# Rows of u and B in the product operands: 3 partitions apart over both halves, loaded 36 at a time

## The reference

```python
def step(h, ins):
    x_t, dt_t, B_t, C_t = ins
    dA = jnp.exp(dt_t[..., None] * A)
    h = dA * h + dt_t[..., None] * B_t[:, None, :] * x_t[..., None]
    y_t = jnp.einsum('ben,bn->be', h, C_t)
    return (h, y_t)
```

## Time and profile before

| | us |
|---|---|
| median of 3 runs | 1169.29 (1166.89 to 1173.1) |
| profiled execution | 1161.89 |
| its span | 1160.1 |
| busy: PE / DVE / ACT / POOL | 1013.9 / 936.7 / 910.1 / 845.2 |
| first update of the state (L1226) starts at | 182.4 |
| last update starts at | 1131.0 |

### The profile page before, as it was taken

One profiled execution on the slowest core, in us unless ns is written; L12 is line 12 of the kernel. 1 busy time (PEld: TensorE's weight loads), 2 busy tenths in 40 slices (PEclk: granted clock), 3 DMA queues, 4 the chain that ended last, 5 costly groups with the idle time before them and its releaser, 6 DMA issues.

```text
span 1160.1 us, 27892 instructions
## 1 busy us (share of the span) xinstructions
PE 1013.9 (87%) x8006; PEld 435.1 (38%) x8006; DVE 936.7 (81%) x2130; ACT 910.1 (78%) x1093; POOL 845.2 (73%) x1215
## 2 busy tenths in 40 slices
PE   5988865699999989897999986999998898899997
PEld 3656521123434333333343332434343333243436
DVE  5667645788989889896999976879897899698983
ACT  1775684888989889886999886879897999788971
POOL 5465405687888878786888875778787888688880
PEclk9999985558989999998999988889899899798999
DMA  4243469999999999998999997989999899999940
GB/s 134 105 147 130 172 226 294 326 319 316 315 317 334 321 327 329 319 330 303 304 347 324 334 306 281 320 270 345 318 341 331 305 337 327 286 328 323 334 154 10
DMA packets 77140, 327.38 MB, mean 282 GB/s; under 512 B 13856, under 2 KB 33184, under 8 KB 41888
## 3 DMA queue, kind: packets, MB, share of 16 engines
q1 hardware_dynamic: 76960, 325.31, 83.0%
HBM read 303.24 MB, written 22.02 MB: 280 GB/s over the span
## 4 chain that ended last, share of the span: by engine, by line
PE 33%; DVE 23%; POOL 14%; issue 14%; DMA 8%; ACT 4%; SPq 3%; DVEq 1%; ACTq 0%; POOLq 0%
PE ps L793 11%; POOL decayed L588 9%; DVE ps L1215 8%; PE ps L738 7%; DMA decay<-dt_stage 7%; PE ps L878 6%; DVE state L1226 6%; PE ps L892 4%; DVE h L1330 2%; ACT state L1025 2%; SPq L392 1%; DVE soft L1142 1%; POOL soft L539 1%; DVE h L1339 1%; SPq L190 1%
## 5 line engine op out<-in xcount | busy, mean ns | idle before, releaser
L588 POOL TENSOR_TENSOR decayed<-decay,state 128x256 f32<-128x256 f32 x1024 | 726.3, 733 | 215.6 <-DVE state L1226 172.6
L1005 ACT ACTIVATE decay<-decay,a_col 128x2048 f32<-128x2048 f32 x256 | 512.6, 2003 | 65.8 <-DMA decay<-dt_stage 52.0
L1226 DVE TENSOR_TENSOR state<-decayed,ps 128x256 f32<-128x256 f32 x1024 | 399.8, 417 | 62.6 <-POOL decayed L588 31.8
L1215 DVE TENSOR_TENSOR ps<-decay,ps 128x512 f32<-128x512 f32 x512 | 352.7, 689 | 73.9 <-ACT state L1025 33.9
L793 PE MATMUL ps<-state,c_cols 128*32 128x256 f32 x4096 | 362.3, 429 | 0.0
L1025 ACT COPY state<-ps 128x512 f32<-128x512 f32 x512 | 289.0, 581 | 91.0 <-issue 47.6
L738 PE MATMUL ps<-moving,b_rows 36*128 36x256 bf16 x1024 | 214.9, 293 | 98.1 <-DVE ps L1215 94.1
L745 PE MATMUL ps<-moving,b_rows 36*128 36x256 bf16 x1024 | 216.0, 294 | 13.7 <-DMA b_rows<-b_stage 13.7
L878 PE MATMUL ps<-h,w 128*128 128x256 f32 x512 | 188.6, 456 | 1.0 <-DVE h L1330 0.8
L738 PEld LDWEIGHTS ps<-moving,b_rows 36*128 36x128 bf16 x1024 | 58.8, 96 | 286.8 <-DVE ps L1215 169.1
L793 PEld LDWEIGHTS ps<-state,c_cols 128*32 128x32 f32 x4096 | 84.2, 112 | 122.9 <-issue 104.6
(11 more groups left out here) (122 smaller groups left out, 823.7 us busy)
## 6 DMA issues: line engine op xcount, KB each, us to landing
decay<-dt_stage SPq DMA_DIRECT2D x512, 512.0 KB, 7.1
moving<-u_stage SPq DMA_DIRECT2D x64, 288.0 KB
b_stage<-b_parts SPq DMA_DIRECT2D x24, 384.0 KB, 3.8
b_rows<-b_stage SPq DMA_DIRECT2D x128, 72.0 KB
dt_stage<-dt_tok SPq DMA_DIRECT2D x8, 512.0 KB, 3.1
u_stage<-u_parts SPq DMA_DIRECT2D x8, 512.0 KB, 3.1
x_tok<-in_L_attn_x_dram SPq DMA_DIRECT2D x4, 512.0 KB, 3.6
u_stage<-u_parts SPq DMA_DIRECT2D x8, 256.0 KB, 2.1
```

The source lines that it names most:

```text
L588: nc.gpsimd.tensor_tensor(decayed[:, p], decay[:, dec_slot(m, k), p, k % TS, :], state[:, (k - 1) % RING, p * E:(p + 1) * E], ALU.mult).th ...
L1005: nc.scalar.activation(pair, pair, ACT.Exp, scale=a_col[:, 2:3]).then_inc(decay_ready, 1)
L1215: nc.vector.tensor_tensor(ps[:, acc_bank(m, k), :].rearrange("p (q e) -> p q e", q=HQ), decay[:, dec_slot(m, k), HQ:Q, k % TS, :], ps[:, a ...
L1226: nc.vector.tensor_tensor(state[:, k % RING, p * E:(p + 1) * E], decayed[:, p], ps[:, SELFP + k % 2, p * E:(p + 1) * E], ALU.add).then_inc ...
```

## The change

The rows that hold a product now lie three partitions apart. For hq = 0 they are partitions 10, 13, ..., 61 (self half) and 64, 67, ..., 115 (acc half), for hq = 1 one partition further. A matmul runs over all 64 partitions of its half; those without a row hold zeros in `b_rows`, and `moving` is cleared as well. The DRAM stages are laid out so that one DMA takes both halves: u and B each by two loads of 36 rows per chunk, one per hq.

```diff
-    PROWS = NP * NP * 2
-    UROWS = NP * NP * HALF
-    assert UROWS <= HROW
+    ROWS = NP * NP * HALF
+    RSTEP = 3
+    RFIRST = HROW + RSTEP - 1 - RSTEP * (ROWS // 2)
...
-    u_stage = nc.dram_tensor("u_stage", (B, NP, T, E), BF16, kind="Internal").ap()
+    u_stage = nc.dram_tensor("u_stage", (HQ, HQ, 2, NP, T, E), BF16, kind="Internal").ap()
...
-    b_stage = nc.dram_tensor("b_stage", (B, NP, NP, T, 2 * N), BF16, kind="Internal").ap()
+    b_stage = nc.dram_tensor("b_stage", (HQ, HQ, 2, NP, NP, T, 2 * N), BF16, kind="Internal").ap()
...
-        def load_u(sp, t, cb):
-
-            for f in range(2):
-                r0 = f * HROW
-                sp.dma_start(moving[r0:r0 + UROWS, cb].rearrange("r t e -> r (t e)"),
-                             u_stage[f * HALF:(f + 1) * HALF, :, bass.ds(t, TC), :]
-                             .rearrange("b i t e -> (b i) (t e)")
-                             .unsqueeze(1).broadcast_to([HALF * NP, NP, TC * E])
-                             ).then_inc(chunk_loaded[cb], 16)
-
-        def load_b(sp, t, cb, pairs):
-
-            for pair in pairs:
-                r0 = (pair // HQ) * HROW + (pair % HQ) * PROWS
-                sp.dma_start(b_rows[r0:r0 + PROWS, cb, pair % HQ].rearrange("r t n -> r (t n)"),
-                             b_stage[2 * pair:2 * pair + 2, :, :, bass.ds(t, TC), :]
-                             .rearrange("b i j t n -> (b i j) (t n)")
-                             ).then_inc(b_loaded[cb], 16)
+        def product_rows(hq):
+
+            first = RFIRST - 2 + hq
+            return slice(first, first + RSTEP * (ROWS - 1) + 1, RSTEP)
+
+        def load_u(sp, t, cb, hq):
+
+            sp.dma_start(moving[product_rows(hq), cb].rearrange("r t e -> r (t e)"),
+                         u_stage[hq, :, :, :, bass.ds(t, TC), :].rearrange("f b i t e -> (f b i) (t e)")
+                         .unsqueeze(1).broadcast_to([HALF * NP, NP, TC * E])
+                         ).then_inc(chunk_loaded[cb], 16)
+
+        def load_b(sp, t, cb, hq):
+
+            sp.dma_start(b_rows[product_rows(hq), cb, hq].rearrange("r t n -> r (t n)"),
+                         b_stage[hq, :, :, :, :, bass.ds(t, TC), :].rearrange("f b i j t n -> (f b i j) (t n)")
+                         ).then_inc(b_loaded[cb], 16)
...
-                        load_u(sp, t0 + TC, 1)
-                        load_b(sp, t0 + TC, 1, range(0, 2))
+                        load_u(sp, t0 + TC, 1, 0)
+                        load_b(sp, t0 + TC, 1, 0)
                     next_dt(*range(TS, 5, TS))
                     if not first:
-                        load_b(sp, t0 + TC, 1, range(2, Q))
+                        load_u(sp, t0 + TC, 1, 1)
+                        load_b(sp, t0 + TC, 1, 1)
...
+                    nc.gpsimd.memset(moving[:, 0], 0.0)
                     nc.gpsimd.memset(b_rows[:, 0], 0.0).then_inc(rows_zeroed, 1)
...
-                    return slice(f * HROW, f * HROW + UROWS)
+                    return slice(f * HROW, (f + 1) * HROW)
...
+                    nc.vector.memset(moving[:, 1], 0.0)
                     nc.vector.memset(b_rows[:, 1], 0.0).then_inc(rows_zeroed, 1)
```

More of the change, by code:

```diff
@@ L46, in mamba_and_binary_mlp_block @@
     HROW = P // 2
-    PROWS = NP * NP * 2
-    UROWS = NP * NP * HALF
-    assert UROWS <= HROW
+    ROWS = NP * NP * HALF
+    RSTEP = 3
+    RFIRST = HROW + RSTEP - 1 - RSTEP * (ROWS // 2)
+    assert RFIRST > 0 and HROW + HQ - 1 + RSTEP * (ROWS // 2) <= P
     QE = Q * E
@@ L340, in mamba_and_binary_mlp_block @@
         SELFP, FA, ACCP, YP, FB = 0, 2, 3, 6, 7
-        LOADS = 2
+        LOADS = HQ
         def chunks(eng, body):
@@ L404, in store @@
                     for at, (parts, stage, i0, i1, ready) in enumerate(
-                            [(u_parts, u_stage[n], 0, 2, "u_mid_ready")]
-                            + [(b_parts, b_stage[n, i], 0, NP, "b_split") for i in range(NP)]
-                            + [(u_parts, u_stage[n], 2, 3, "u_split")]):
+                            [(u_parts, u_stage[q % HQ, q // HQ, bb], 0, 2, "u_mid_ready")]
+                            + [(b_parts, b_stage[q % HQ, q // HQ, bb, i], 0, NP, "b_split") for i in range(NP)]
+                            + [(u_parts, u_stage[q % HQ, q // HQ, bb], 2, 3, "u_split")]):
                         if n == B - 1 and at == 1:
@@ L431, in _ @@
                     sp.wait_ge(S[f"parts_stored{bb}"], Q * (16 * STORES))
-                load_u(sp, 0, 0)
-                load_b(sp, 0, 0, range(Q))
+                for hq in range(HQ):
+                    load_u(sp, 0, 0, hq)
+                    load_b(sp, 0, 0, hq)
                 for c in range(EARLY, NDEC):
                     load_dt(c, c, [])
-                load_u(sp, TC, 1)
-                load_b(sp, TC, 1, range(Q))
+                for hq in range(HQ):
+                    load_u(sp, TC, 1, hq)
+                    load_b(sp, TC, 1, hq)
                 sp.wait_ge(S["z_ready"], B)
@@ L479, in body @@
                         wait_all(sp, [(acc_state, t0 + TC + 1)])
-                        load_u(sp, t0 + STEPS, 0)
-                        load_b(sp, t0 + STEPS, 0, range(0, 2))
+                        load_u(sp, t0 + STEPS, 0, 0)
+                        load_b(sp, t0 + STEPS, 0, 0)
                     next_dt(*range(16 + TS, 21, TS))
                     if not last:
-                        load_b(sp, t0 + STEPS, 0, range(2, Q))
+                        load_u(sp, t0 + STEPS, 0, 1)
+                        load_b(sp, t0 + STEPS, 0, 1)
                     next_dt(*range(20 + TS, STEPS + 1, TS))
@@ L752, in wait_chunk @@
                         pe.wait_ge(chunk_loaded[cb], (i + k // STEPS + 1) * (16 * LOADS))
-                        pe.wait_ge(b_loaded[cb], (i + k // STEPS + 1) * (16 * Q))
+                        pe.wait_ge(b_loaded[cb], (i + k // STEPS + 1) * (16 * HQ))
                 def self_first():
```

## The result

The changed kernel takes 1117.59 us (1113.17 to 1124.49, 4 runs) where the kernel before, on the same chip, took 1170.72: a ratio of 0.9554, 95% interval 0.9496 to 0.9613. Run a second time on another occasion it was 1109.08 against 1167.54, 0.9535 (0.9463 to 0.9606). The forecast was 1137, with a range down to 1120: the right way, but 20 us too little. The gain is 53 us where I had 32.

A forecast was written before the change was run, and what follows sets the result against it. The prediction took a just about full DMA queue, slowed by u and B loads, as the bound. Its terms -33.5 - 2.6 + 1.5 = -34.6, taken as -32, gave 1137 us from 1169.29; range 1120 to 1163.

The forecast's parts named there:

- Narrow destinations slow the queue, and the queue is full: DMA queue in the scan: u and B on neighbouring partitions slow packets; spreading them removes most decay waits, -33.5 us.
- -33.5 - 2.6 + 1.5: Sum over the kernel: decay waits removed, earlier first product, added DVE memset; together -34.6 us.
- a shading to -32: Whole kernel: the summed -34.6 us cut to -32, since some would be lost to the next engine in line.
- part 4: PE's 2048 products over 64 rows instead of 36: instruction length about unchanged, 0 us, bounds -12 and +12.
- body 13: A 32-step scan body, 64.1 us, 9.0 over the short one, with 9.6 of ACT's waits for decay.
- The rival's 0.38 us per microsecond: TensorE's clock: each microsecond at 0.50 costs 0.38 us, so 108 us more low time costs +41; chance 0.07.
- Start of the scan: First chunk's loads on SP: issues end sooner and transfers are quicker, so the first product comes earlier, -2.6 us.
- Memsets: End of the prologue: DVE's extra clearing of moving costs +1.5 us, POOL's is hidden by idle time.
- Order on SP: SP's issues in the scan: the second u load goes behind two pairs of decay loads; 0, no more than -1 us.
- The source: Chunk loads: widely spaced source rows in the stages cause the dips, so they stay; 1170 us, chance 0.13.
- Something else takes the place: Scan: decay waits go, but engines wait for each other or the clock is lower more often; 1157 us, chance 0.12.
- The clock on the wrong side: TensorE: products over 64 rows lower the granted clock, +41 against -32, giving 1178 us; chance 0.07.

The follow-up runs named there:

- dense destinations: Changed kernel with its four loads per chunk going to 36 neighbouring partitions instead of every third: 1195.49 us, ratio 1.0228.
- one source row: Kernel before, with all rows of a u or B load reading the same row of their stage: 1166.24 us, ratio 0.9976.
- one-row loads: Kernel before, each u and B load carrying one row from the third chunk on: 1130.40 us; with products over 64 rows and both memsets, 1104.65 us.
- the two other orders: Changed kernel with its four chunk loads parted by pairs of decay loads, 1130.72 us, or all ahead of the decay loads, 1105.46 us.

## Why the prediction was wrong in its size

1. *Narrow destinations slow the queue, and the queue is full.* The cause is right, and shown: dense destinations bring the dips and the waits back (1195), one source row doesn't remove them (0.998). The size came out near, in part by luck. Relieving the queue with 36-row products gave -34, against -33.5 - 2.6 + 1.5 and a shading to -32, but by one-row loads, which also leave bytes out (spread rows with 36-row products can't be had, since they fill the half). Taking the 26 us of part 4 off the 53 and 58 us of the two measurements leaves 27 to 32 for the spread, an estimate. The steps to that number were wrong. The queue doesn't empty: it moves 347 to 351 GB/s while busy instead of 338, so a body's transfers went from 55.6 to about 54 us, not to 46. Behind the loads it makes 279 to 300 GB/s, not 350. The waits for `decay` left over are 26.0 and 10.6 us in two executions, not 2, and landing fell by 0.5 us, not 2. The worth of a wait was also misread: body 13, whose 9.0 us over the short body were all put down to waits, ran at a clock of 0.87, so 2 x 0.13 x 64.1 = 17 us of it were at the lower level. That a small relief is enough, because the queue was only just over its limit, is argued and not shown.

2. *Products over 64 rows: 0, bounds -12 and +12.* This is the step that failed. I priced the instruction, whose length doesn't change, and not the clock, and took the clock up only as a rival that makes it slower. Its sign was wrong: with more rows in each product the clock is low for less of the time, 228 to 133 us with the loads as before, 185 to 82 with one-row loads, and there it is worth 26 us. That is beyond the bound of -12 as well, and it is more than the 20 us that the forecast was short of. The mean clock of 0.960 lies above the 0.87 to 0.95 that the forecast allowed.

3. *The price of low clock.* The rival's 0.38 us per microsecond was too high for what it stood for: 26 us in the median for 103 us less is 0.25. The profiled executions of that pair, with 70 us less and 12.0 us between their spans, give 0.17. And with the loads as before 95 us less brought nothing, so it isn't a constant: it depends on what else is at its limit.

4. *Start of the scan.* -2.6 forecast, -1.3 found (8.4 to 7.2 us): a strided B load takes SP 0.79 us to issue, not 0.5. *Memsets:* +1.5 forecast, +1.0 found, POOL's hidden. *Order on SP:* 0 forecast; SP still stands 173.7 us waiting for states, so it isn't short of time. That order can matter was not foreseen: the two other orders stand at 0.9711 and 0.9502.

5. *Rivals.* The source (0.13) is refuted. "Something else takes the place" (0.12) was the wrong way about: the clock was low less often, not more often, and the change moved both limits at once. The clock on the wrong side (0.07) had the right quantity with the wrong sign.

What stays open: why the number of rows moves the clock (only that it does is shown), what holds the rate behind spread loads under 415 GB/s, and why the order of the loads counts. By the port map of the Trainium skill ("SBUF — State Buffer", Door 1) the 36 rows reach all 16 ports both two and three apart. The runs agree in that both are equally fast and dense rows are slow. The map doesn't say why the dense version is slower than the kernel before. No run here tries rows that are far apart and share a port, so the map itself isn't tested.

The Trainium skill's rule on how many engines a copy uses ("DMA: Bandwidth & Descriptors", Why a DMA increments its semaphore by 16) can be checked after all. The profile page's count of packets under 512 B, of before and of the changed kernel:

```profile
DMA packets 77140, 327.38 MB, mean 282 GB/s; under 512 B 13856, under 2 KB 33184, under 8 KB 41888
```

```profile
DMA packets 76758, 327.39 MB, mean 294 GB/s; under 512 B 13472, under 2 KB 32800, under 8 KB 41504
```

384 small packets fewer. By the rule, with one completion packet for each DMA engine used, B goes from 128 loads x 9 to 64 x 12, which is 1152 - 768 = 384; u is the same. The trace agrees. The one-row loads with 36-row products bear out the 12 of u as well: 30 chunks x (2 x 12 + 4 x 9), less one packet for each of the six one-row loads that take their place, is 1800 - 180 = 1620 fewer than before. That run has 12236 small packets, which is 1620 fewer.

## What to carry to other kernels

A load's destination is a term of its cost: when DMA engines are fully busy at half their usual rate, look where the rows land, and try to spread them before touching their number. When a kernel has two limits near each other (a full queue and a low clock here), removing one alone may show nothing, so test them two by two; a null result of one doesn't clear it. And when a change alters how much of the matrix engine a product fills, its price is read from the granted clock, not only from the length of the instruction.

## What the runs showed of the hardware that was not expected

- Rows of zeros are not free of effect and not costly either: products over 64 partitions instead of 36 run at the same 266 ns at best, and the time at the lower of the two clock levels falls from 185 to 82 us of the span with one-row loads, in the median of four executions each.
- The clock also rises when the DMA queue is relieved and the products stay as they are: from 0.90 to 0.918 with 36 rows, from 0.943 to 0.963 with 64.
- Issuing a DMA of 36 rows of B takes SP 0.38 us to neighbouring partitions and 0.78 us to every third one (first the dense version, then the changed kernel):

```profile
610.44 0.38 SPq L200 DMA_DIRECT2D b_rows<-b_stage  x1
```

```profile
613.11 0.78 SPq L201 DMA_DIRECT2D b_rows<-b_stage  x1
```
